# Gate and up products of an FFN's first layer, made record by record in turn into two PSUM banks

## The reference

```
x = x + attention(layernorm(x), context)     # 8 heads of 32, causal mask of 256 x 77
h = silu(y @ w1.T * s1) * (y @ w2.T * s2)    # y = layernorm(x); gate and up, 256 -> 1024
h = gelu(h @ h1.T * t1)                      # 1024 -> 1024
h = gelu(h @ h2.T * t2)                      # 1024 -> 1024
x = x + (h @ w3.T * s3)                      # 1024 -> 256
```

## Time and profile before

| | |
|---|---|
| Runs shown | 1680.45 us median of 3 (1677.08 to 1680.65) |
| Profiled execution | 1678.55 us |
| Its span, first to last instruction | 1676.8 us |
| Mean granted TensorE clock | 0.986 of 2.4 GHz |
| PE busy | 1623.1 us, 97% |
| DVE, ACT, POOL busy | 833.1, 731.8, 137.8 us |
| FFN matmuls (L333) in the chain that ended last | 69% |

### The profile page before, as it was taken

One profiled execution on the slowest core, in us unless ns is written; L12 is line 12 of the kernel. 1 busy time (PEld: TensorE's weight loads), 2 busy tenths in 40 slices (PEclk: granted clock), 3 DMA queues, 4 the chain that ended last, 5 costly groups with the idle time before them and its releaser, 6 DMA issues.

```text
span 1676.8 us, 22220 instructions
## 1 busy us (share of the span) xinstructions
PE 1623.1 (97%) x8970; PEld 1311.3 (78%) x8970; DVE 833.1 (50%) x1421; ACT 731.8 (44%) x1121; POOL 137.8 (8%) x136
## 2 busy tenths in 40 slices
PE   4499999999999999999999999999999999999998
PEld 3378888787887878788787887878888787887887
DVE  5672644637355462644637355462644637355331
ACT  4453443535345353443535345353443535345342
POOL 1100102010020200102010020200102010020000
PEclk8699999999999999999999999999999999999999
DMA  7100001000000100001010000100001010000000
GB/s 302 62 7 26 29 0 54 0 29 25 25 29 0 41 13 25 29 1 53 0 28 26 25 29 0 41 13 25 29 2 52 0 32 22 25 29 1 1 13 13
DMA packets 17206, 48.39 MB, mean 29 GB/s; under 512 B 5536, under 2 KB 7584, under 8 KB 15648
## 3 DMA queue, kind: packets, MB, share of 16 engines
q1 hardware_dynamic: 17184, 48.09, 8.1%
HBM read 39.63 MB, written 8.45 MB: 29 GB/s over the span
## 4 chain that ended last, share of the span: by engine, by line
PE 86%; DVE 8%; issue 3%; ACT 2%; DMA 1%; POOL 0%; DVEq 0%; SPq 0%; POOLq 0%; ACTq 0%
PE ffn_banks L333 69%; PE att_banks L469 4%; PE att_banks L486 3%; PE att_banks L441 3%; DVE a_lo L644 2%; PE att_banks L478 2%; PE att_banks L434 2%; DVE a_f L639 2%; DVE mx L678 2%; DVE probs L674 1%; PE att_banks L429 1%; PE att_banks L360 1%; PE att_banks L458 1%; ACT a_f L516 1%; DVE stage L632 1%
## 5 line engine op out<-in xcount | busy, mean ns | idle before, releaser
L333 PE MATMUL ffn_banks<-a_hi,h_sb 128*128 128x512 f32 x1024 | 408.5, 399 | 0.0
L333 PE MATMUL ffn_banks<-b_hi,h_sb 128*128 128x512 f32 x1024 | 401.3, 392 | 0.0
L333 PE MATMUL ffn_banks<-a_lo,h_sb 128*128 128x512 f32 x1024 | 400.0, 391 | 0.0
L333 PE MATMUL ffn_banks<-b_lo,h_sb 128*128 128x512 f32 x1024 | 398.6, 389 | 0.0
L650 DVE TENSOR_TENSOR a_lo<-a_f,a_hi 128x512 fp32r<-128x512 f32 x128 | 88.6, 692 | 317.8 <-ACT a_hi L531 317.8
L530 ACT ACTIVATE a_f<-ffn_banks,vec 128x512 f32<-128x512 f32 x128 | 88.3, 690 | 354.1 <-PE ffn_banks L333 354.1
L333 PEld LDWEIGHTS ffn_banks<-a_hi,h_sb 128*128 128x128 f32 x1024 | 192.3, 188 | 45.9 <-issue 6.2
L650 DVE TENSOR_TENSOR b_lo<-b_f,b_hi 128x512 fp32r<-128x512 f32 x128 | 85.8, 689 | 285.9 <-ACT b_hi L531 285.9
L333 PEld LDWEIGHTS ffn_banks<-b_lo,h_sb 128*128 128x128 f32 x1024 | 192.3, 188 | 39.8
L333 PEld LDWEIGHTS ffn_banks<-b_hi,h_sb 128*128 128x128 f32 x1024 | 192.3, 188 | 39.8
L333 PEld LDWEIGHTS ffn_banks<-a_lo,h_sb 128*128 128x128 f32 x1024 | 192.5, 188 | 38.2
(11 more groups left out here) (87 smaller groups left out, 1935.8 us busy)
## 6 DMA issues: line engine op xcount, KB each, us to landing
x_in<-in_x SPq DMA_DIRECT2D x16, 512.0 KB, 3.6
stage<-in_h SPq DMA_DIRECT2D x8, 1024.0 KB, 14.1
out<-out_sb SPq DMA_DIRECT2D x16, 512.0 KB, 2.6
ln_t<-in_x_t SPq DMA_DIRECT2D x15, 512.0 KB, 4.4
ln_rows<-ln_rows_dram SPq DMA_DIRECT2D x15, 512.0 KB, 3.9
stage<-in_w SPq DMA_DIRECT2D x3, 1024.0 KB, 9.3
ctx_sb<-in_ctx_t SPq DMA_DIRECT2D x16, 154.0 KB, 3.8
w_att_sb<-in_w_att SPq DMA_DIRECT2D x1, 1024.0 KB, 7.3
```

The costliest lines, as they stand in the source:

```text
L333: mm = nc.tensor.matmul(psum, left, right, start=(k == 0 and part == 0), stop=(k == rows - 1 and part == 1))
```

## The change

In the branch that runs, the 8 matmuls of a product are issued in another order. Before: the four of the gate, then the four of up. After: for each of the two blocks and each part (hi, lo) one matmul of the gate and one of up. The order of the four adds within a bank stays. The waits for both banks, which stood ahead of the gate half (`silu_done`) and of the up half (`up_used`), stand ahead of the product together. `gate_ready` is raised by the seventh matmul and no longer by the fourth, `up_ready` by the eighth as before. Products of L2, L3 and L4, and all other engines, are unchanged.

```diff
+            def two_products(banks, weights, rows, hi, lo):
+
+                for k in range(rows):
+                    for part, x_ap in enumerate((hi(k), lo(k))):
+                        last = []
+                        for bank, w_sb in zip(banks, weights):
+                            last.append(nc.tensor.matmul(bank, w_sb(k), x_ap, start=(k == 0 and part == 0),
+                                                         stop=(k == rows - 1 and part == 1)))
+                return last
+
...
-                        for i, (w_sb, used, ready) in enumerate(((w1_sb, silu_done, gate_ready), (w2_sb, up_used, up_ready))):
-                            if n >= 2:
-                                pe.wait_ge(used, KH * f + n - 1)
-                            bank = fb[:, 2 * (n % 2) + i, :]
-                            hi, lo = (lambda k: ln2_hi[:, k, :]), (lambda k: ln2_lo[:, k, :])
-                            if general:
+                        if n >= 2:
+                            pe.wait_ge(silu_done, KH * f + n - 1)
+                            pe.wait_ge(up_used, KH * f + n - 1)
+                        banks = [fb[:, 2 * (n % 2) + i, :] for i in range(2)]
+                        hi, lo = (lambda k: ln2_hi[:, k, :]), (lambda k: ln2_lo[:, k, :])
+                        if general:
+                            for i, (bank, ready) in enumerate(zip(banks, (gate_ready, up_ready))):
                                 product_general(bank, c0 + KD * i, f, KD, hi, lo, None, 0)
                                 signal(ready, general)
-                            else:
-                                product(bank, lambda k: w_sb[:, k, n * P:(n + 1) * P], KD, hi, lo, None, 0).then_inc(ready, 1)
+                        else:
+                            gate, up = two_products(banks, [lambda k, w_sb=w_sb: w_sb[:, k, n * P:(n + 1) * P]
+                                                            for w_sb in (w1_sb, w2_sb)], KD, hi, lo)
+                            gate.then_inc(gate_ready, 1)
+                            up.then_inc(up_ready, 1)
```

## The result

The changed kernel takes 1687.15 us in the median (7 runs, 1683.89 to 1688.49), the kernel before 1678.76 us in runs beside it (7 runs, 1677.08 to 1682.51). The ratio is 1.0045, 95% interval 1.0036 to 1.0054, that is 7.6 us slower (6.0 to 9.1), with 6.9 forecast. The two medians by themselves lie 8.4 us apart. The profiled execution of the changed kernel has a span of 1686.7 us, 9.9 more than that of before.

A forecast was written before the change was run, and what follows sets the result against it. PE, busy 97% and waiting at S3 for the DVE chain, was taken as the bound. 15 × 0.46 = 6.9 us, other terms 0, gave 1685.4 from the profiled execution or 1687.3 from the median; 1686.5 taken, range 1680.5 to 1691.

The forecast's parts named there:

- The bound: First layer, passes 0 to 14: PE waits at score step S3 for DVE's mask, already open by 0.19 us per pass.
- (a): Product 3: gate bank finished three matmuls later delays silu, DVE chain and S3 by 0.46 us per pass, 6.9 us.
- The others' silu is free: Products other than 3: silu moves by up to 0.69 us at no cost; silu 5 is nearest.
- (b): Up bank's wait moved to a product's first matmul: just touches at product 6, 0.24 us left in pass 15; taken as 0.
- the two waits on one instruction: Waits ahead of a product: two on one instruction cost nothing, as S0 carries three and follows in 0.31 us.
- (c): Neighbouring matmuls using different banks and weights: bounded by 11 ns gain or 13 ns loss each, taken as 0.
- the rule of the Trainium skill: Gate and up banks falling due together lose evacuation overlap: the whole 0.69 us per pass, 10.4 us.
- Same-bank cost and late chain: Rival: turning banks saves 11 ns per matmul, 0.34 us up to product 3's seventh; net +1.1 us, chance 0.10.
- S3's lateness was PE's own: Rival at S3: PE's own sequencing, not the mask, makes it late; 11.3 us could be gained, 1669, chance 0.05.
- The chain gave nothing back: Rival on DVE: something in its chain gives back over half of the 0.46 us, no change; chance 0.12.
- The signs in the profile: Pass profile: silu 3 at about 13.5 us, S3 0.96 us behind product 7, starts 0.227 apart, no multiply wait over 0.1.
- The 4.5 us of idling ahead of the multiply: DVE ahead of product 3's multiply: idling of 4.5 us, not 4.04.

The follow-up runs named there:

- e5: Changed kernel with gate and up in turn in product 3 alone, the other products gate half first, both waits in front; pass 101.016 us.
- e3: Changed kernel in the order gate, up, gate, gate, gate, up, up, up, so the gate is complete with the fifth matmul; pass 100.56 us.
- e9: Changed kernel with the four up matmuls first, then the four of the gate, complete with the eighth; pass 101.243 us.
- e4: Changed kernel, but product 3 alone has its gate half first as before, its waits still in front; pass 100.633 us.
- e2: Changed kernel in the order gate, up, gate, up, gate, gate, up, up, the gate complete with the sixth matmul; pass 100.79 us.
- e11: Changed kernel, S3 after four matmuls of L2's product 0, DVE's row maximum and subtraction of S2 behind a_lo of product 7; pass 100.425 us, ratio 0.9987.
- e10: Kernel before, S3 after two matmuls of L2's product 0, DVE's row maximum and subtraction of S2 behind a_lo of product 7; pass 100.406 us, ratio 0.9987.
- e7: Kernel before, with PE alone doing S3 after the first two matmuls of L2's product 0, not ahead of them; 0.09 us gained per pass.

## Why the prediction was right

- **The bound.** "Whatever delays the DVE chain's head from here on delays PE in full": silu 3, its multiply, the mask and S3 came 0.45, 0.45, 0.44 and 0.45 us later. The forecast was 0.46. e5 shows that product 3 alone is that head.
- **(a), 0.46 us per pass, 6.9 us.** 0.455 measured, 6.8 us in 15 passes. That 0.23 us of the delay hide behind the q bias was the step that a count of three matmuls (0.69 us) would have missed; e3 and e9 show both sides of it, free at the fifth place and 0.23 us for every place after it.
- **The others' silu is free.** Right in the changed kernel. Its reason, that the multiply of product 5 has itself moved by then, was needed: in e4, where it has not moved, 0.07 us appear.
- **(b), 0, was too small.** "It just touches": product 6 was held by 0.08 us, which S3's lateness hides. In pass 15, where 0.24 us of slack were reckoned, 0.15 us were lost (14.69 us for the eight products against 14.53). Two terms of that sum were off. The wait stands on the weight load and not on its matmul, and the load starts 0.22 us ahead of it. And from the end of the multiply to that load it is 0.12 us and not the 0.05 read at the mask. With both, by the terms of the prediction, 2.26 − 0.22 = 2.04 us stand against 0.39 + 0.04 + 0.79 + 0.75 + 0.12 = 2.09: each load comes some 0.05 us late. The place is product 2 of pass 15, changed kernel (the multiply of product 0, the last loads of product 1, the first load and matmuls of product 2):

```profile
1602.61 0.75 DVE L653 SCALAR_TENSOR_TENSOR a_f<-ffn_banks,vec,a_f 128x512 f32<-128x512 f32 x1 [1.71 <-ACT a_f L530]
...
1602.98 0.41 PEld L343 LDWEIGHTS ffn_banks<-ln_lo,w_sb 128*128 128x128 f32 x2
...
1603.48 0.37 PEld L343 LDWEIGHTS ffn_banks<-ln_hi,w_sb 128*128 128x128 f32 x2
...
1603.66 0.62 PE L343 MATMUL ffn_banks<-ln_hi,w_sb 128*128 128x512 f32 x2
```

The up bank is free at 1602.61 + 0.75 = 1603.36, the load starts at 1603.48; PE's loading stands idle for 0.09 us ahead of it (1602.98 + 0.41 = 1603.39), where 0.04 us is usual. Products 3 to 7 have the same 0.12 us between multiply and load. e2, complete with the sixth matmul, loses nothing there (14.53). Whether the two waits on one instruction, which the prediction counted as nothing, make the difference between 0.05 and 0.12 us is open.
- **(c), 0.** Right: the distance stayed 0.227 us, and e11 comes within 0.02 us of e10. The 13 ns over the 512 columns stay unexplained; they are not a matter of the bank.
- **By the rule of the Trainium skill**, Perfetto Trace Analysis, section Matmuls, as the prediction read it, the loss was to be 0.69 us per pass. The page names no size; the 0.69 are the three matmuls of the rows. The trace agrees in the direction: the measured 0.455 is the 0.69 less what ACT was busy with.
- **The rivals.** Same-bank cost and late chain would have made silu 3 come at 13.2; it came at 13.52. That S3's lateness was PE's own is out: it moved with the mask, 0.05 to 0.06 us behind its end again (209.05 + 0.79 = 209.84 to 209.90), and in e7 it is gone. The chain gave nothing back.
- **The signs in the profile.** Silu 3 at 13.52 (13.5 forecast), S3 0.93 us behind product 7's last matmul (0.96), 0.227 us between the starts, no wait for the multiply over 0.1 us: these came. The 4.5 us of idling ahead of the multiply did not; it was 3.93, since the prediction moved the multiply of product 3 and left DVE's work for product 2 where it was. Nothing else in the sum rests on it.
- **The number.** 1686.5 was taken between 1685.4 and 1687.3; 1687.15 was measured. That the two agree so closely is partly luck: the forecast leaned on a median of 1680.45 for the kernel before, which with four more runs is 1678.76, 1.7 us lower, and the medians differ by 8.4 us and not by 6.9. The effect per pass, 0.455 against 0.46, is the better test.

## What to carry to other kernels

Count the matmul that signals, not the matmuls: an order that keeps every matmul and every distance still moves the moment at which another engine may start, by one matmul for each place. Look then for the engine whose list has no idle time between that moment and PE's next wait; the delay passes through it whole, less what its reader was busy with anyway. When a wait is taken away from such a chain, look up who else reads the chain's end (here a_lo of product 7) before counting the gain. And count the slack of a wait up to the weight load that carries it, here 0.22 us ahead of the matmul.

## What was not expected of the hardware

After the idle place in pass 0 (3.5 us) the granted clock of the next microseconds is 0.50 in some executions and 1.00 in others of the same stretch, which goes with 1.6 to 2.8 us in pass 0. From 95 us of the span to 1670 the granted clock was 1.00 in all 13 executions profiled here, those with 0.6 us of idling at S3 in each pass included. And the distance of matmuls needs some ten of them to come back to 0.227 us after a score step (0.34, 0.24, 0.24, 0.23 as above). In pass 15 of the changed kernel, where the loads come some 0.05 us late, it does not come back at all: products 2 to 7 follow each other in 1.82 to 1.85 us, in the kernel before in 1.81 to 1.82. A load that waits for one semaphore starts 0.05 us after DVE's instruction ends (the mask before S3, a_lo in L2), the one with two waits 0.12 us after.
